# Row sends of the last two batches issued one at a time, between exponentials and tile results

## The reference, cut to what matters

```python
x = L0_attn_x                                   # (8, 512, 128) f32
x = _layernorm(x + _L0_attn_ref(x, ...))        # 16 heads, causal, scale 1/sqrt(128)
# in _L0_ffn_ref, on x of all 4096 tokens:
logits = x @ gate_w.T                           # (4096, 14)
probs = jax.nn.softmax(logits, axis=-1)
top2_p, top2_i = jax.lax.top_k(probs, 2)
w = top2_p / jnp.maximum(top2_p.sum(-1, keepdims=True), 1e-10)
hh = jax.nn.gelu(jnp.einsum('nd,edf->nef', x, w1) + b1, approximate=False)
all_out = jnp.einsum('nef,efd->ned', hh, w2) + b2
result = jnp.clip(x + w[:, 0:1] * out0 + w[:, 1:2] * out1, -100.0, 100.0)
x = _layernorm(x + result)
```

## Time and profile before

| | us |
|---|---|
| median of 3 runs | 441.88 |
| lowest and highest run | 439.37, 444.35 |
| span of the profiled execution, first to last instruction | 510.3 |
| busy in the span: PE, DVE, ACT, POOL | 420.0, 349.9, 327.5, 287.8 |

### The profile page before, as it was taken

The page is one execution under the profiler, slowest core; times in us unless marked ns, Lnnn a source line. Parts: engine busy times, 40 slices in busy tenths (PEclk is TensorE's granted clock), DMA queues, the critical chain, the costliest instruction groups (busy, mean ns, idle before and its releaser), DMA issues.

```text
span 510.3 us, 21148 instructions
## 1 busy us (share of the span) xinstructions
PE 420.0 (82%) x8602; PEld 310.1 (61%) x8602; DVE 349.9 (69%) x910; ACT 327.5 (64%) x776; POOL 287.8 (56%) x483
## 2 busy tenths in 40 slices
PE   7696999998898899898898888496567787967991
PEld 2363566675585585585585455165557676866991
DVE  7984888997697697697698696256634454533286
ACT  5293887977777777777776657165446666655435
POOL 6032344557657657657657667524765665665542
PEclk9998999999999999999999999789668889888996
DMA  6644375565466466544444312501434333237134
GB/s 190 192 120 143 116 202 159 186 185 168 152 173 186 148 185 168 162 140 130 148 125 120 87 30 52 135 13 40 109 106 110 89 81 83 78 76 231 49 117 125
DMA packets 77664, 65.24 MB, mean 128 GB/s; under 512 B 12390, under 2 KB 72045, under 8 KB 77568
## 3 DMA queue, kind: packets, MB, share of 16 engines
q1 hardware_dynamic: 72624, 55.27, 38.4%
q0 software_dynamic: 4512, 8.54, 5.0%
q10 hardware_dynamic: 432, 0.07, 0.1%
HBM read 36.88 MB, written 25.46 MB: 122 GB/s over the span
## 4 chain that ended last, share of the span: by engine, by line
PE 57%; DVE 12%; issue 9%; ACT 6%; SPq 6%; another core or an unknown queue 5%; DMA 2%; POOL 2%; DVEq 0%; ACTq 0%; POOLq 0%
PE psum L1099 19%; PE psum L1191 11%; PE psum L1133 8%; PE psum L1354 6%; DVE nmax L1533 6%; PE psum L1369 5%; ACT probs L952 4%; PE psum L1440 3%; SPq L513 2%; PE psum L1146 2%; PE psum L1343 2%; PE psum L1432 1%; SPq L538 1%; DMA dq<-side 1%
## 5 line engine op out<-in xcount | busy, mean ns | idle before, releaser
L952 ACT ACTIVATE probs<-psum 128x512 f32<-128x512 f32 x320 | 182.5, 598 | 80.4 <-PE psum L1099 52.3
L1533 DVE TENSOR_REDUCE nmax<-psum 128x2 f32<-128x1024 f32 (+7 forms) x256 | 180.4, 746 | 50.5 <-remote 29.3
L1099 PE MATMUL psum<-qst,kst 128*32 128x128 bf16 (+3 forms) x2048 | 149.3, 303 | 22.6 <-issue 12.9
L836 POOL TENSOR_SCALAR_AFFINE_SELECT probs<-probs 128x512 f32<-128x512 f32 x180 | 81.8, 484 | 107.8 <-ACT probs L952 107.8
L1133 PE MATMUL psum<-kst,qst 128*32 128x288 bf16 (+15 forms) x2048 | 105.6, 281 | 7.1 <-DVE nmax L1533 4.0
L915 POOL DMA_INDIRECT o_dram<-probs,xs x77 | 77.6, 1007 | 58.4 <-DVE probs L1793 34.2
L1191 PE MATMUL psum<-probs,vst 128*32 128x256 f32 (+2 forms) x1280 | 105.6, 386 | 4.2 <-issue 3.5
L1099 PEld LDWEIGHTS psum<-qst,kst 128*32 128x32 bf16 x2048 | 61.0, 96 | 70.5 <-issue 35.3
L1146 PE MATMUL psum<-bmask,bident 128*32 128x64 bf16 (+2 forms) x1280 | 76.7, 198 | 0.8 <-issue 0.8
L1133 PEld LDWEIGHTS psum<-kst,qst 128*32 128x32 bf16 x2048 | 60.4, 96 | 21.2 <-issue 7.0
L1146 PEld LDWEIGHTS psum<-bmask,bident 128*32 128x32 bf16 x1280 | 45.1, 97 | 10.0 <-issue 2.8
(11 more groups left out here) (245 smaller groups left out, 690.8 us busy)
## 6 DMA issues: line engine op xcount, KB each, us to landing
kst<-dk SPq DMA_DIRECT2D x62, 128.0 KB, 3.5
qst<-dq SPq DMA_DIRECT2D x31, 256.0 KB, 4.4
xs<-xs_dram SPq DMA_DIRECT2D x77, 66.0 KB
dk<-side SPq DMA_DIRECT2D x7, 384.0 KB
dq<-side SPq DMA_DIRECT2D x7, 384.0 KB, 2.8
dk<-side SPq DMA_DIRECT2D x9, 256.0 KB, 3.0
side<-in_xT SPq DMA_DIRECT2D x8, 256.0 KB, 3.4
dq<-side SPq DMA_DIRECT2D x8, 256.0 KB, 2.7
```

The lines of the kernel that those rows point to most:

```text
L836: pool.affine_select(out=view, in_=view, compare_op=ALU.is_ge, fill=0.0, base=0, pattern=[[0, view.shape[1]], [1, P]], channel_multiplier= ...
L952: act.activation(probs[:, c % 2, p, kk * T:(kk + 1) * T], psum[:, km_bank(b, c, k), :], ACT.Exp, scale=SCALE).then_inc(S["exp_done"], 1)
L1099: last = pe.matmul(out[32 * g:32 * g + 32], stationary[:, 32 * g:32 * g + 32], moving, skip_group_check=True, **flags)
L1533: last = dve.tensor_reduce(nmax[:, c, 2 * t:2 * t + 2], ps[:, :, at:at + TWO * (t + 1)], AX.X, ALU.max, negate=True)
```

## The change

Batch 6's sends: one stays at place (2, 1) of pass 7; the second goes to (3, 0) behind five exponentials of group 3, the third to (3, 1) behind all ten; the other five go one each behind results 0 to 4 of pass 8. Batch 7's eight sends alternate with results 7 to 14. All of it is on POOL; the other engines' programs are the same, and no DMA is added or dropped.

```diff
         LAST = {
             "scatter": {(0, 0): (0,), (0, 1): (1, 2), (1, 0): (3, 4), (1, 1): (5, 6), (2, 0): (7,)},
-            "early": {(2, 1): range(TOPK * NQ)}}
+            "early": {(2, 1): (0,), (3, 0): (1,), (3, 1): (2,)},
+            "behind_exps": {(2, 1): 0, (3, 0): 5, (3, 1): NBANK}}
+        EARLY_SENT = 3
...
                             if closing(b) and (c, p) in LAST["early"]:
+                                pool.wait_ge(S["exp_done"], n + LAST["behind_exps"][c, p])
                                 send(b - 1, 1 - odd, LAST["early"][c, p])
...
                     if c == 0 and b == B:
-                        put_out(0, OUT_AHEAD)
+                        for j in range(OUT_AHEAD):
+                            put_out(j, j + 1)
+                            send(b - 2, odd, (EARLY_SENT + j,))
...
                     if c == 3 and b == B:
-                        send(b - 1, 1 - odd, range(TOPK * NQ))
+                        for n in range(TOPK * NQ):
+                            send(b - 1, 1 - odd, (n,))
+                            put_out(OUT_FIRST + n, OUT_FIRST + n + 1)
...
-            put_out(OUT_FIRST, NT)
+            put_out(OUT_FIRST + TOPK * NQ, NT)
```

## The result

The changed kernel takes 450.03 us (median of 4 runs, 447.37 to 451.11) beside 443.12 us for the kernel before (4 runs, 439.37 to 445.71): a ratio of 1.0167, 95% interval 1.0121 to 1.0212, or 7.4 us more by the ratio (so are all differences below). Forecast was 445.7 us, that is +3.8. The direction was right, the size half of what came, and the time lies 0.03 us above the range's end of 450.0. Of the 4.3 us between forecast and time, 1.2 are the base: the kernel before stood at 441.9 us in the prediction and has 443.12 here.

A forecast was written before the change was run, and what follows sets the result against it. The prediction took a chain mostly on PE, with POOL hardly on it but its power L852 without slack, as the bound. It summed 441.9 + 2.8 + 0 + 1.0 - 0 = 445.7 us, range 437.0 to 450.0.

The forecast's parts named there:

- What bounds the kernel: Whole span: the chain that ended last is 57% PE, 12% DVE, 2% POOL, so POOL is hardly on it.
- Batch 6's first three sends cost nothing: POOL before result 0: one send stays, two fill the 11.67 us idle stretch, at no cost.
- The power is late by 2.8 us, at most 4.8: POOL's power L852: ten DMAs now precede it, so it starts near 352.4 rather than 349.65; bounds 0 and 4.8 us.
- the one pause of 2.0 us: DVE's y, 346.10 to 348.10, waiting for another core or unknown queue; if missing unprofiled, L852's delay is 4.8 us.
- The delay goes through to the end: Behind L852: DVE's offset, PE's ranks and ACT's layer norm wait without slack, so 2.8 us reach the end.
- Interleaving saves nothing, and costs 1.0 us of at most 2.7: Batch 7's sends: earlier result 7 wins nothing; POOL idles before result 9, bounds 0 and 2.7 us, taken as 1.0.
- The burst was real: Rival, chance 0.22: PE's stall beside batch 6's sends is real, 9 us come back, giving 436.7 us.
- POOL is the bound without the profiler: Rival, chance 0.22: from L852 on POOL sets the pace; 4.8 and 2.7 us count whole, giving 449.4 us.
- Nothing moves: Rival, chance 0.14: L852's delay is absorbed by later unprofiled adds or a longer wait behind it, leaving 441.9 us.

The follow-up runs named there:

- clean trace: The kernel before, unchanged, traced a second time; the run took 441.6 us with a span of 439.9 us.

## Why the prediction was half right

*What bounds the kernel.* Wrong, and the step that failed first. "POOL, which the change alone touches, is hardly on the chain" was read from the earlier trace rows of a trace that was 68 us longer than the runs. The prediction said that it distrusted stretched stretches, and then used the stretch's waits of the earlier trace rows as the measure of POOL's slack. In a clean trace POOL has none from result 7 to the last: no idle time over 0.31 us, and four short instructions put there cost 4.5 us. So the sum priced a delay (2.8) and a part of one wait (1.0), and left out that the 6.4 us of issue, which the prediction itself had worked out for the five late sends, find hardly any idle time of POOL to fill.

*Batch 6's first three sends cost nothing.* Right: in the changed kernel result 0 waits for its add, not for a send, and it is 6.2 us behind the last exponential as in the clean trace of before (6.3).

*The power is late by 2.8 us, at most 4.8.* The mechanism was right, the size wrong. It is 5.7 us late (12.93 against 7.25 us behind result 0), more than the upper bound. The ten DMAs took 12.9 us, about the 12.8 that were worked out; but in the clean trace vpe starts 6.84 us behind result 0 and not 9.59 as in the first trace, which lost 2.75 us there, more than the one pause of 2.0 us that the upper bound had taken away.

*The delay goes through to the end.* The sum charged the delay of the power alone. The runs show two costs: 6.4 us of issue time that used to lie in an idle stretch, and the idle time before batch 7's copy that the late power keeps open. With the power on time (five sends behind it) +4.9 us stay (+2.8 in the trace); with the power almost on time and the alternation kept, +3.0 (+2.3).

*Interleaving saves nothing, and costs 1.0 us of at most 2.7.* The first half was right: SP's load of tile 23 stands behind the pad stores, at 338.81 in the changed kernel, 14 us after result 7. The idle time before result 9 was foreseen to 0.2 us (2.7 against 2.90), but it counted in full, +3.8 us (2.3 to 5.3) by the runs. Taking 1.0 "nearer to the row" was the mis-sized term.

*The burst was real.* Refuted by the second trace of before: the same burst, no stall. The argument from SP's register moves held: a stall that hits work without transfers belonged to that one recording. Why that one execution was recorded so slowly stays open; none of the ten later ones was.

*POOL is the bound without the profiler.* This rival was the case, +7.5 us against +7.4: POOL has no slack, and the delays of the power and of result 9 count in full. That the number is so near is in part luck. Its terms were 4.8 us of delay and 2.7 us of idle time, the ledger's are 6.4 us of issue and 2.1 us of idle time, and its pitch of 1.28 us is 1.32 in the clean trace (77 DMAs from 316.27 to 418.13). It was given 0.22, less than a forecast that rested on the doubtful waits. The argument for it, a pitch of 1.28 us a result against 1.0 us that PE takes for a tile, came from rows that no pause had touched, and should have carried more weight than a sum of waits.

*Nothing moves.* Refuted: the whole interval lies 5.4 us and more above before.

The Trainium skill (Runtime: NRT & Kernel Launch, The ~15µs preamble/postamble breakdown) puts the gap between a profile's total and the reported time at 6.2 us. It doesn't explain the first trace, whose span is 68.4 us above the runs. The changed kernel's span is 1.8 us below its time; but a span from first to last instruction need not be the total that the rule means, so this doesn't test it.

## What to carry to other kernels

Set a trace's span beside the run's time before reading anything else; if it is much longer, its waits are no measure of slack; the usual length and pitch of POOL's DMAs (0.97 and 1.28 us) were the same in the stretched trace and the clean one. An engine that issues DMAs can be the bound by its pitch times its count while its busy share looks low. Work moved from its idle stretch into its full one then costs about its whole time, and each wait that it meets in order is lost. In such a queue put what is ready first, and the one small instruction that others wait for ahead of everything that may be late.

## What the runs showed of the hardware

Most indirect DMAs on POOL take 0.97 us, and some up to 1.4 us. In the second trace of before two long ones (325.82 and 327.49 above) lie beside DVE's fetches of 0.50 us, with adds in turn:

```profile
325.74 0.50 DVE L1784 COPY w_cur<-experts 128x642 f32 x1
326.15 0.28 DVE L1793 TENSOR_TENSOR probs<-psum,w_cur 128x128 f32<-128x128 f32 x1
326.57 0.50 DVE L1784 COPY w_cur<-experts 128x642 f32 x1
```

What counts is how soon behind such a copy's start the DMA starts. In the ten traces other than the first of before, the 38 DMAs that start 0.08 to 0.12 us behind one take 1.21 to 1.37 us, the 39 that start 0.18 to 0.22 us behind one 1.11 to 1.16, and of the 79 that start 0.35 us or more behind one none takes over 1.05, though the copy still runs. Not every long one is of this sort: the DMA right behind the power takes 1.12 us without such a copy, and the longest of the changed kernel, 1.41 us at 422.41, has other work of DVE beside it.

The Trainium skill (SBUF — State Buffer, Who interferes with whom) says that DVE in a 2-port mode and GpSimd share a pair of ports, of which the second to come is blocked until the first has finished. That a DMA which starts early in a copy loses most agrees with it; that these copies run in such a mode is not shown, and no run here took them away.

Two traces of one kernel differed by 70 us of span (510.3 and 439.9 us), the longer with register moves of up to 703 ns that else take at most 39. A change's profile alone would have been read as 61 us faster, while its runs are 7 us slower.
